# Reloaded blocks of one step multiplied jointly, up to three per product, in a two-layer graph network

## What is computed

```
coeff = w_comp[etype]
msg = einsum('ebo,eb->eo', einsum('ei,bio->ebo', x[src], weight), coeff) * edge_weight[:, None]
x1 = layernorm(x + relu(segment_sum(msg, dst) + bias))

out = segment_sum(norm[:, None] * (x1 @ W)[src with loops], dst with loops)
y = layernorm(x1 + out + b)
```

## Time and profile before

| | us |
|---|---|
| median of three runs | 2065.78 |
| lowest and highest | 2060.22, 2066.22 |
| the profiled execution | 2064.73 |
| its span in the trace | 2063.1 |

### The profile page before, as it was taken

One profiled execution on the slowest core, in us unless ns is written; L12 is line 12 of the kernel. 1 busy time (PEld: TensorE's weight loads), 2 busy tenths in 40 slices (PEclk: granted clock), 3 DMA queues, 4 the chain that ended last, 5 costly groups with the idle time before them and its releaser, 6 DMA issues.

```text
span 2063.1 us, 62174 instructions
## 1 busy us (share of the span) xinstructions
PE 1504.5 (73%) x22006; PEld 1221.6 (59%) x22006; DVE 1286.3 (62%) x3606; ACT 857.4 (42%) x2171; POOL 1496.8 (73%) x1590
## 2 busy tenths in 40 slices
PE   3785666666666677677778787777887788888887
PEld 2554545544554565566556566656766676776776
DVE  7885555755566655575565576565756656576546
ACT  5563443543434344343434354343444434344303
POOL 7777777777777777777777777777777777777720
PEclk7888787877888888898888899899999999999987
DMA  5544443444334544545444444455345554455593
GB/s 133 155 147 148 140 147 95 139 127 134 101 118 136 156 128 148 158 128 145 136 139 122 137 142 150 135 153 154 108 146 153 166 143 117 141 171 151 169 387 108
DMA packets 195126, 300.01 MB, mean 145 GB/s; under 512 B 66230, under 2 KB 132459, under 8 KB 188687
## 3 DMA queue, kind: packets, MB, share of 16 engines
q1 hardware_dynamic: 93736, 162.31, 22.1%
q10 hardware_dynamic: 50983, 82.41, 13.1%
q0 software_dynamic: 50112, 51.41, 12.8%
HBM read 187.43 MB, written 108.56 MB: 143 GB/s over the span
## 4 chain that ended last, share of the span: by engine, by line
PE 38%; POOL 23%; issue 18%; DMA 9%; DVE 5%; ACTq 3%; ACT 2%; SPq 1%; POOLq 1%; DVEq 0%
POOL gathered_rows L787 23%; DMA gathered_rows<-in_x,idx 7%; PE coefs_ps L1341 5%; PE types_ps L1217 4%; PE node_ps L1217 4%; PE sums_ps L1217 4%; PE dense_ps L1217 3%; PE coefs_ps L1307 3%; PE sums_ps L1241 3%; PE sums_ps L1254 3%; ACTq L614 2%; ACT room L1019 1%; PE node_ps L1227 1%; DVE first_room L1832 1%; PE sums_ps L1318 1%
## 5 line engine op out<-in xcount | busy, mean ns | idle before, releaser
L787 POOL DMA_INDIRECT gathered_rows<-in_x,idx x1559 | 1476.9, 947 | 477.2 <-issue 421.5
L1241 PE MATMUL sums_ps<-gathered_rows,chunk_factors 128*32 128x64 f32 x3118 | 98.3, 253 | 408.1 <-issue 204.4
L1832 DVE TENSOR_TENSOR first_room<-first_room,dve_ps 128x1024 bf16<-128x1024 bf16 x585 | 365.2, 680 | 0.0
L1241 PEld LDWEIGHTS sums_ps<-gathered_rows,chunk_factors 128*32 128x32 f32 x3118 | 63.0, 124 | 423.2 <-issue 208.2
L1019 ACT COPY room<-dense_ps 128x294 f32 x390 | 168.8, 433 | 320.4 <-PE dense_ps L1217 270.7
L1854 DVE TENSOR_TENSOR dve_ps<-coefs_ps,edges 128x32 f32<-128x32 f32 x196 | 38.8, 198 | 338.4 <-PE coefs_ps L1202 334.6
L948 ACT COPY parts<-sums_ps 128x128 f32<-128x128 f32 x196 | 52.0, 265 | 463.8 <-PE sums_ps L1241 449.6
L1019 ACT COPY room<-node_ps 128x294 f32 x390 | 168.8, 433 | 180.3 <-PE node_ps L1217 59.8
L1826 DVE TENSOR_TENSOR first_room<-dve_ps,first_room 128x1960 bf16<-128x1960 f16 (+2 forms) x260 | 238.8, 939 | 0.0
L1217 PE MATMUL dense_ps<-first_room 128*128 128x245 bf16 x1170 | 217.9, 300 | 27.8 <-DVE first_room L1832 27.8
L1217 PE MATMUL sums_ps<-first_room 128*128 128x245 bf16 (+1 forms) x1170 | 233.8, 312 | 0.0
(11 more groups left out here) (300 smaller groups left out, 2518.9 us busy)
## 6 DMA issues: line engine op xcount, KB each, us to landing
acc_room<-block_table ACTq DMA_DIRECT2D x147, 374.5 KB
block_table<-room SPq DMA_DIRECT2D x11, 2621.5 KB
type_rows<-in_edge_type SPq DMA_DIRECT2D x260, 96.0 KB
gathered_rows<-in_x,idx POOLq DMA_INDIRECT x1559
block_table<-room SPq DMA_DIRECT2D x9, 2247.0 KB
acc_room<-block_table ACTq DMA_DIRECT2D x56, 321.0 KB, 4.1
block_table<-room SPq DMA_DIRECT2D x9, 1872.5 KB
block_table<-room SPq DMA_DIRECT2D x10, 1498.0 KB
```

Of the source, the lines that this page charges most:

```text
L787: pool.indirect_dma_start(gathered_rows[:, s, j, 0:D], None, rows, bass.IndirectOffsetOnAxis(ap=idx[:, s, j:j + 1], axis=0)).then_inc(rows ...
L1241: last = nc.tensor.matmul(parts_ps[lane:lane + LANE, D * k:D * k + D], chunk_factors[:, q, c, :], rows, start=True, stop=True)
L1832: last = nc.vector.tensor_tensor(lo_hot[:, w, q0:q1, :, :], lo_hot[:, 2, q0:q1, :, :], part_of_weights(w), ALU.mult)
```

## The change

Units of one step that belong to the same batches are taken in one joint visit. A product then has the same stationary tile of x1 and, as moving operand, the 107 columns of that tile of two or three units (a pattern with one stride of a slot). Their partial sums, where there are any, still go in one by one. The units must lie in neighbouring slots, so the slots are no longer given by round robin: for a joint visit of n units the planner takes the run of n neighbouring open slots whose latest user is the longest ago, and the first such run where several are equal. `unit_read`, on which the loads of the next users of the slots wait, is raised by n at the end of the joint visit instead of by one after each unit. The late visits are as before.

```diff
+def joint_visits(step):
+
+    runs = []
+    for u in range(BEGUN[step], BEGUN[step + 1]):
+        if runs and UNITS[runs[-1][0]][1:3] == UNITS[u][1:3]:
+            runs[-1][1] += 1
+        else:
+            runs.append([u, 1])
+    return runs
...
-                v = u % sum(freed_by <= opened for freed_by in FREED_BY)
+                if u == u0:
+                    places_open = sum(freed_by <= opened for freed_by in FREED_BY)
+                    v0 = min(range(places_open - n + 1), key=lambda a: max(free_at.get(a + m, -1) for m in range(n)))
+                v = v0 + u - u0
...
+            def sum_units_of_blocks(u0, n, at):
+
+                b, k, end, _ = UNITS[u0]
+                to = coefs_ps[:, at:at + n * VISIT].rearrange("p (n w) -> p n w", w=VISIT)
+                units = plane[:, slot_of[u0] * SLOT:(slot_of[u0] + n) * SLOT].rearrange("p (n w) -> p n w", w=SLOT)
+                begun = False
+                for u in range(u0, u0 + n):
+                    pe.wait_ge(unit_loaded[slot_of[u]], loads_until[u])
+                    if UNITS[u][3]:
+                        nc.tensor.matmul(to[:, u - u0, 0:WB], ident[:, :], partial_of(u), start=not begun, stop=False, skip_group_check=True)
+                        begun = True
+                tiles = FIRST_TILE[end] - FIRST_TILE[k]
+                for t in range(tiles):
+                    side = t % 2 * D
+                    last = nc.tensor.matmul(to[side:side + D, :, 0:WB], x_nodes[:, FIRST_TILE[k] + t, 1:D + 1], units[:, :, t * WB:(t + 1) * WB],
+                                            start=(not begun and t < 2), stop=(t >= tiles - 2), skip_group_check=True)
+                last.then_inc(unit_read, n)
...
-                        for u in range(BEGUN[step], BEGUN[step + 1]):
-                            sum_unit_of_block(u, visit_ps[u - BEGUN[step]])
+                        for u0, n in joint_visits(step):
+                            sum_units_of_blocks(u0, n, VISITS_AT + (u0 - BEGUN[step]) * VISIT)
```

More of the change, by code:

```diff
@@ L168, with joint_visit @@
 SLOTS = 27
+def joint_visits(step):
[6 more added lines that the diff above has]
+    return runs
+def joint_visit(u):
+    step = next(n for n in range(ITERS * U) if BEGUN[n + 1] > u)
+    return next((step, u0, n) for u0, n in joint_visits(step) if u0 <= u < u0 + n)
 COMPLETES = [max(n for n, (b, _, _, _) in enumerate(REST) if b < at) for at in TURNED_AT]
@@ L357, in gnn_two_layers @@
             if u < BEGUN[-1]:
-                step = next(n for n in range(ITERS * U) if BEGUN[n + 1] > u)
+                step, u0, n = joint_visit(u)
                 opened = max(e for e in QUOTA if TURNED_AT[e] + 2 <= step // U)
-                v = u % sum(freed_by <= opened for freed_by in FREED_BY)
+                if u == u0:
+                    places_open = sum(freed_by <= opened for freed_by in FREED_BY)
+                    v0 = min(range(places_open - n + 1), key=lambda a: max(free_at.get(a + m, -1) for m in range(n)))
+                v = v0 + u - u0
             else:
@@ L403, in gnn_two_layers @@
         node_ps = pb("node_ps", [P, 512])
-        visit_ps = [coefs_ps[:, at:at + WB] for at in (176, 284, 392)]
+        VISITS_AT, VISIT = 176, 108
+        visit_ps = [coefs_ps[:, at:at + WB] for at in range(VISITS_AT, VISITS_AT + 3 * VISIT, VISIT)]
         dense_ps = [pb("dense_ps", [P, 512]), node_ps, types_ps, sums_ps[2]]
```

## The result

The changed kernel takes 2070.71 us (median of 14 runs, 2066.50 to 2079.52), the kernel before beside it 2065.11 us (14 runs): ratio **1.0035**, 95% interval 1.0023 to 1.0047. A ratio is taken over all executions and not from the two medians, which differ by 5.6 us; on 2065.78 us the ratio means about 7 us more. Left out of its ratio is one execution only, of the first kernel under "The experiments", which took 6632.73 us where the other eleven took 2064 to 2071; nothing recorded tells why. The forecast of 2068.0 us had the right sign and a third to two fifths of the size: 2.2 us were forecast. The time lies in the range of 2061 to 2074, and the ratio just on the "slower" side of 0.3%. The profiled execution of the changed kernel has a span of 2071.8 us, against 2063.1. It is one of the longer ones, 2.7 us above the median, so its 8.7 us are more than the kernels differ by.

What follows compares the result with a forecast made beforehand. POOL's unbroken gathers were taken to bound the loop. Late-load stalls of 5.3 us, less 1.6 saved and 1.5 absorbed at the end, gave 2.2 us on 2065.78: 2068.0 us, range 2061 to 2074.

Steps and rivals of the forecast that it cites:

- the "slower" side of 0.3%: Whole kernel: time up by more than 0.3%, 6.2 us, beyond what can be told from no change; chance 0.13.
- POOL sets the loop: Whole loop: POOL gathers without a break, 195 steps of 8 at 1.25 us, whatever PE does.
- The reading of the chain of waits: Rival for the loop: PE, 38% of the chain, sets its length; 5.1 us would go, 2060.7; faster had chance 0.04.
- A joint record costs 139 ns: Loop visits: 321 columns at 2.4 GHz plus 5.4 ns; saves 5.1 us of PE time, 1.6 in steps 177 to 188.
- The cover: Loop up to 1950 us and its end: PE's 5.1 us saved lie beside POOL's gathers and become waiting; worth 0.
- When the third load lands: Steps 177 to 188: third load issued 0.9 us after the first, landing 5.0 us after the first issue.
- How long PE stands: Steps 179, 180, 182, 183, 185 stall 1.0 us each, 186 0.3, 177 nothing: 5.3 us in all.
- Step 188's trade is 0: Steps 188 and 189: eight DMAs issued instead of one delay PE about as much as step 189 wins back; 0.
- POOL isn't held up: From 400 us on: PE's 3.7 us of lateness stays under the tightest margin, 7.0 us at step 179.
- 1.5 us vanish at the end: Loop's end: of 3.7 us lateness, 1.46 disappear in PE's wait for gathered rows before 1961.42; 2.2 us remain.
- slower by the long stall: Rival in steps 177 to 188: stalls of 2.0 us instead of 1.0 add 8.2 us, time 2074; chance 0.13.

Runs made afterwards that it cites:

- the first kernel under "The experiments": Changed kernel's slots and loads, late ones included, but products taken one by one, against the kernel before: 2068.38 us, 1.0011.
- 738 records fewer: Kernel before with its round robin slots and loads, units multiplied jointly only where they happen to be neighbours: 2065.26 us, 0.9999.
- with seven gathers: Eighth gather of each step left out in iterations 20 to 64, against the kernel before: separate products 0.9385, joint with early loads 0.9370, changed kernel 0.9448.
- with fillers: Changed kernel plus four unused 64-column products ahead of the visit's wait in the seven stalling steps: 2069.84 us, 1.0018 of the kernel before.
- the kernel with early loads: All the change's joint products, but slots chosen by smallest sum of latest uses and loads begun once their slot is free; against the kernel before: 2067.07 us, 1.0010.
- the kernel with two tiles: Kernel before with two tiles instead of up to seven in each loop visit, 1938 of 2770 records left out: 2064.62 us, 0.9996.

## Why the forecast came out as it did, step by step

**POOL sets the loop: right.** The rate and the 1.25 us of a gather are unchanged, and a kernel with 1938 records fewer is no faster. The reading of the chain of waits that spoke against it, 38% PE, would have been wrong.

**A joint record costs 139 ns: wrong, 149.** Of the chain of waits:

```profile
1960.02 1.78 PE coefs_ps L1382 x12
```

1.78 us for twelve, where 36 single ones take 1.80. I took the 5.4 ns between 44.6 and 50 as a price of a record, which three columns' worth of records would pay once. It turns out to go with the columns: 321 / 2.4 is 134 ns, and the record takes 149, 11% more, just as 50 is 12% above 44.6. The other row for this, three of 343 columns in 0.46 us, stood in the same sum: 153 ns, 7% above its columns, and scaling by columns gave 143 from it. I took the lower of two estimates. Term: 1.6 us were to be saved in steps 177 to 188; measured 0, and 1.1 us of busy time over the whole loop where 5.1 were forecast. By "TensorE: Matmul & The Clock Gate" of the Trainium skill, "Back-to-back issue gap", 131 ns for 512 columns, the joint record should have been faster still; the run shows 149 ns for 321.

**The cover: right.** With POOL setting the pace, 738 records fewer give 0.9999. Even where PE sets it, with seven gathers, the records removed are worth less than four executions can tell.

**When the third load lands: right.** 5.0 us after the first issue were forecast. From the first issue to the visit it is 5.2 us in step 179, 5.1 in 180, 5.2 in 182 and in 183, and 6.0 in 185, from 1857.40 to 1863.43. Steps 177 and 186 have 6.0 and 5.5.

**How long PE stands: the mis-sized term.** 5.3 us were forecast, 8.5 measured. The five steps that I named make 1.07 + 1.05 + 1.17 + 1.16 + 1.96 = 6.4 for 5.0. The rest is in two steps that I had cleared by the time at which PE wanted its data before: step 177 (0.91 for 0), where a partial sum's load goes between the first and the second block, so that the third lands 6.0 us after the first, and step 186 (1.15 for 0.3), where PE wanted it 4.3 us after the first issue and not 4.7, and it came after 5.5 and not 5.0. What stayed at step 188 are 7.6 us: the 0.91 of step 177 had been made up by step 179.

**Step 188's trade is 0: wrong by a little, as far as lateness tells.** Lateness rises by 5.3 us at step 189 and falls by 3.8 at 190: 1.5 us stay. With slots and loads alone 3.2 stay, with fillers 1.9. In the kernel with early loads, which issues six DMAs in step 188 and not eight, 0.5 stay.

**The clock: not in the sum at all.** The visit at 1863.43 took 1.4 us more than its neighbours, and the dense products behind 1880.50 took 0.79 instead of 0.49 us; over steps 179 to 187 PE was busy for 3.0 us longer. A wait was priced at its own length; that PE was slower after it was left out, and no reason given. Before the end it shows again: the last block takes 6.06 us against 4.41 in the earlier trace rows, 1.7 us more. The wait ahead of it, 3.18 us, is hardly longer than the 2.94 us before, so the length of a wait alone doesn't say whether the clock falls.

**POOL isn't held up: wrong by a little.** A margin of 7.0 us was read at step 179, where lateness was still 0; the place that counted was step 191, behind all stalls, with 14.0 us of lateness. It cost 1.9 us once. The last gather's start, which was to stay within 1 us of 1959.8, moved by 4.6; 2.5 of that are the offset from the loop's start.

**1.5 us vanish at the end: right, but outweighed.** The wait for gathered rows is gone; the slower last block takes its 1.5 us back. The rows forecast for 1963 to 1964 begin at 1974.11.

With what was measured in place of what was forecast, the sum is 7.6 (stalls) + 3.0 (clock, steps 179 to 187) + 1.5 (step 188) + 1.7 (clock, last block) - 1.5 (vanished) - 0 (saved) = 12.3 us, where the trace has 12.7 at these rows. The stalls came where they were forecast, for the reason that was forecast. They were under-sized, the saving was over-sized, and two costs stood in the sum at nothing: the clock and step 188's trade.

That 2.2 us forecast and 5.6 to 7 us measured are no further apart is in part luck. PE was to be 3.7 us late at step 188 and was 10.5 in the profile. The tail then gave 3.9 us back, which the forecast didn't have, and 2.5 us of offset from the loop's start may be in the profile's figures. The rival "slower by the long stall" came nearer in size, with 8.2 us, by a wrong route: stalls of 2.0 us each, of which there was one.

## What to carry to other kernels

A product over several blocks waits for the last of them. Before joining products, look at when each operand lands, and price the join as the lateness of the last, not as a saving of instructions; the 940 records saved here took 1.1 us off PE's busy time, since the price went with the columns. A planner that picks storage by "longest ago used" can quietly turn loads that were a step ahead into loads in the step of use: its choice must be read together with the loads' times. And when a term of the sum is a margin, read it at the place where the lateness has piled up, not where the margin is smallest today.

## What the runs showed of the hardware that I had not expected

- An f32 record of 107 columns takes 50 ns and one of 321 takes 149 ns at clock 1.00: some 11% above 2.4 GHz at either size.
- Two stalls of about 2 us in PE's work, at 1863 and 1880 us, went with a granted clock of 0.66 to 0.87 in the 5 us around or behind them, in which twelve records took 3.24 us instead of 1.86. With 1.0 us of other products in the first it stayed at 1.00. Not each stall did it: behind 2.94 us without work the last block of the kernel before ran at 1.00 (90 records in 4.41 us), behind 3.18 us that of the changed kernel took 6.06 us. A PE with less to do had less clock in the same 100 us: 0.89 at 77% busy in the kernel with two tiles against 0.97 at 85% in the kernel before.
- The same program takes 2065, 2772 and 2806 us on different chips. Where the kernel before takes 2772 us, the changed kernel starts 59 gathers in 100 us and not 81, so that something else than POOL sets its pace.
